# First attention: q, k and the score maxima in two fp32r parts, scores of 24 and 26 rows in four row tiles

## The reference

```python
qkv = x @ W_qkv
q, k, v = jnp.split(qkv, 3, axis=-1)           # 16 heads of 8 dims
scores = jnp.einsum('bhnd,bhmd->bhnm', q, k) / jnp.sqrt(jnp.float32(128))
attn = jax.nn.softmax(scores, axis=-1)
out = jnp.einsum('bhnm,bhmd->bhnd', attn, v)
x = _layernorm(x + out)
```

## Time and profile before

| | before |
|---|---|
| median of 3 runs | 1043.92 us (1043.27 to 1044.46) |
| span of the profiled execution | 1041.4 us |
| PE busy | 995.5 us (96%) |
| PEld busy | 475.4 us (46%) |
| DVE busy | 834.0 us (80%) |
| ACT busy | 729.9 us (70%) |
| POOL busy | 475.6 us (46%) |

### The profile page before, as it was taken

One profiled execution on the slowest core, in us unless ns is written; L12 is line 12 of the kernel. 1 busy time (PEld: TensorE's weight loads), 2 busy tenths in 40 slices (PEclk: granted clock), 3 DMA queues, 4 the chain that ended last, 5 costly groups with the idle time before them and its releaser, 6 DMA issues. The chain is left out here.

```text
span 1041.4 us, 20120 instructions
## 1 busy us (share of the span) xinstructions
PE 995.5 (96%) x5835; PEld 475.4 (46%) x5835; DVE 834.0 (80%) x1874; ACT 729.9 (70%) x939; POOL 475.6 (46%) x483
## 2 busy tenths in 40 slices
PE   8899999999999999999999999999999999999996
PEld 3222222222222235888888887873332333222485
DVE  6889999999999977787888789897666666643677
ACT  2078777787777786555555555568898888899754
POOL 0332514325053725676777677576442244220275
PEclk9999999999999999999999999999999999999998
DMA  6553222131321003344324323443512331230011
GB/s 198 153 186 119 76 76 89 44 117 46 96 78 52 3 2 101 102 128 145 101 91 156 121 90 117 137 137 102 172 65 61 121 119 63 60 122 1 1 31 52
DMA packets 73981, 97.04 MB, mean 93 GB/s; under 512 B 12669, under 2 KB 42237, under 8 KB 73533
## 3 DMA queue, kind: packets, MB, share of 16 engines
q1 hardware_dynamic: 73928, 96.40, 29.7%
HBM read 68.18 MB, written 27.79 MB: 92 GB/s over the span
## 5 line engine op out<-in xcount | busy, mean ns | idle before, releaser
L741 DVE TENSOR_REDUCE a_nmax<-a_ps_f 128x1 f32<-128x512 f32 x512 | 320.1, 683 | 20.2 <-PE a_ps_f L579 19.7
L497 ACT ACTIVATE a_prob<-a_ps_s 128x1024 f32<-128x1024 f32 x256 | 251.7, 1023 | 77.8 <-PE a_ps_s L646 76.5
L1367 ACT ACTIVATE a_prob<-a_ps_s 128x1024 f32<-128x1024 f32 x256 | 244.4, 1026 | 28.0 <-PE a_ps_s L1419 26.7
L2187 POOL TENSOR_TENSOR moe_hl<-moe_hid,moe_hh 128x512 fp32r<-128x512 f32 x134 | 173.9, 1303 | 84.3 <-ACT moe_hh L2068 84.2
L579 PE MATMUL a_ps_f<-a_ks,a_qs 48*128 48x512 bf16 x512 | 157.9, 386 | 11.8 <-DVE a_nmax L741 4.3
L2058 ACT ACTIVATE moe_ps<-moe_ps 128x512 f32<-128x512 f32 x128 | 74.5, 582 | 111.5 <-PE moe_ps L1981 110.7
L1432 PE MATMUL a_ps_o<-a_prob,a_va 128*32 128x512 f32 x1024 | 136.4, 605 | 1.4 <-DVE a_turned_o L1547 0.5
L659 PE MATMUL a_ps_o<-a_prob,a_va 128*32 128x512 f32 x1024 | 136.4, 605 | 0.5 <-ACT a_prob L497 0.4
L646 PE MATMUL a_ps_s<-a_qs,a_ks 51*128 51x512 bf16 x512 | 132.5, 381 | 1.7 <-ACT a_prob L497 1.5
L579 PEld LDWEIGHTS a_ps_f<-a_ks,a_qs 48*128 48x128 bf16 x512 | 39.7, 93 | 192.2 <-DVE a_nmax L741 162.2
L2109 DVE TENSOR_TENSOR moe_prod<-moe_cw,moe_ps 128x512 f32<-128x512 f32 x128 | 87.2, 681 | 27.4 <-PE moe_ps L1981 26.7
(11 more groups left out here) (302 smaller groups left out, 1640.1 us busy)
## 6 DMA issues: line engine op xcount, KB each, us to landing
moe_cw<-r_weights SPq DMA_DIRECT2D x256, 128.0 KB, 2.9
parts_q<-a_parts SPq DMA_DIRECT2D x48, 256.0 KB, 2.5
parts_k<-a_parts SPq DMA_DIRECT2D x48, 256.0 KB, 2.5
a_qs<-parts_q SPq DMA_DIRECT2D x126, 96.0 KB, 2.4
a_ks<-parts_k SPq DMA_DIRECT2D x126, 96.0 KB, 2.5
a_xt<-in_x_t SPq DMA_DIRECT2D x8, 256.0 KB, 2.8
out_x<-g_X SPq DMA_DIRECT2D x7, 256.0 KB, 2.3
moe_wg<-in_wg SPq DMA_DIRECT2D x1, 1088.0 KB, 6.6
```

What stands on the lines that cost most here:

```text
L497: nc.scalar.activation(prob[:, u % PSLOTS, :, :], ps_s[:, u % 2, :, :], ACT.Exp, scale=float(P) ** -0.5).then_inc(exp_done, 1)
L741: nc.vector.tensor_reduce(nmax[:, half_no, h % 2, col:col + 1], ps_f[:, bank, :], AX.X, ALU.max, negate=True).then_inc(max_done, 1)
L1367: nc.scalar.activation(prob[:, u % PSLOTS, :, :], ps_s[:, u % 2, :, :], ACT.Sigmoid, scale=float(HD) ** -0.5).then_inc(exp_done, 1)
L2187: nc.gpsimd.tensor_tensor(hl[:, part_at(j), :], hid[:, hid_at(j), :], hh[:, part_at(j), :], ALU.subtract).then_inc(hl_done, 1)
```

## The change

q and k are split into two fp32r parts instead of three bf16 parts, and the maxima too. Three pairs of parts remain (24 rows), and two rows of maxima (26). Four heads lie at partitions 0, 32, 64 and 96, so that scores run in four row tiles of 32. `s1_place` changes the order of the heads in the first pass: score n takes head (n + 2) mod 4 of its group. The stacks, the maxima and the selection become fp32r. A group's stack is read by four DMAs for q and four for k (24 rows of 2 KB each), parts are written by two DMAs, the maxima's rows by four. The rows of ones are filled by GpSimd ahead of the first stack, and SP lays them once more into the first group. At the start one selection gives four heads, by two matmuls for q and two for k; its matrix comes as fp32 and GpSimd turns it into fp32r. The V product, the maxima, the exponentials, the order of the units and the three banks stay as they are. The core of the diff:

```diff
 def s1_place(n):
-    return 2 * (n // (2 * NT)) + n % 2, n // 2 % NT
+    return HG * (n // (HG * NT)) + (n + 2) % HG, n // HG % NT

+def quarter_rows(tile, h, n_rows):
+    return tile[QTR * (h % HG):QTR * (h % HG) + n_rows, h // HG, :]
+
+def write_terms(sp, scratch, parts, n, done):
+    dst, src = scratch.rearrange("r p t -> p r t"), parts.bitcast(F32)
+    if n == 0:
+        sp.dma_start(dst[:, 0:2, :], src[:, 0:1, :].broadcast_to([P, 2, T])).then_inc(done, 16)
+        sp.dma_start(dst[:, 2:3, :], src[:, 1:2, :]).then_inc(done, 16)
...
+def read_terms(sp, scratch, dst, grp, done):
+    for i in range(HG):
+        src = bass.AP(tensor=scratch.tensor, offset=(i * NG + grp) * T, ap=[[H * T, FQKR], [1, T]])
+        sp.dma_start(dst[QTR * i:QTR * i + FQKR, grp, :].bitcast(F32), src).then_inc(done, 16)
+
+def split_in_two(eng, ops, src, parts, k, split, parts_done, zero):
+    ops.tensor_tensor(parts[:, 0, :], src, zero, ALU.add).then_inc(split, 1)
+    eng.wait_ge(split, k + 1)
+    ops.tensor_tensor(parts[:, 1, :], src, parts[:, 0, :], ALU.subtract).then_inc(parts_done, 1)
...
             def max_rows(b, p, half_no):
-                for i in range(2):
-                    sp.dma_start(qs[p][HALF * i + QKR:HALF * i + MXR, half_no * HH // 2:(half_no + 1) * HH // 2, :],
-                                 mparts[i * PARTS * HH * NT // 2:(i + 1) * PARTS * HH * NT // 2, :]).then_inc(max_in, 16)
+                rows = MAX_ROWS // HG
+                for i in range(HG):
+                    src = rows_of(half_no).start + i * rows
+                    dst = qs[p][QTR * i + FQKR:QTR * i + FMXR, half_no * NG // 2:(half_no + 1) * NG // 2, :]
+                    sp.dma_start(dst.bitcast(F32), mparts[src:src + rows, :]).then_inc(max_in, 16)
...
-                nc.tensor.matmul(ps_f[:, bank, :], stack_rows(qs[p], h, QKR)[:, qt * P:(qt + 1) * P],
-                                 stack_rows(ks[p], h, QKR), start=True, stop=True).then_inc(s1_done, 1)
+                nc.tensor.matmul(ps_f[:, bank, :], quarter_rows(qs[p], h, FQKR)[:, qt * P:(qt + 1) * P],
+                                 quarter_rows(ks[p], h, FQKR), start=True, stop=True).then_inc(s1_done, 1)
...
-                    mm = nc.tensor.matmul(ps_s[:, u % 2, i, :], stack_rows(ks[p], h, MXR)[:, kt * P:(kt + 1) * P],
-                                          stack_rows(qs[p], h, MXR), start=True, stop=True)
+                    mm = nc.tensor.matmul(ps_s[:, u % 2, i, :], quarter_rows(ks[p], h, FMXR)[:, kt * P:(kt + 1) * P],
+                                          quarter_rows(qs[p], h, FMXR), start=True, stop=True)
...
+            for i in range(2):
+                nc.gpsimd.memset(ks[i][:, :, :].bitcast(F32), 1.0).then_inc(filled, 1)
+            nc.gpsimd.memset(msplit[:, :, :, :, :], 0.0).then_inc(mt_chain, 1)
+            pool.wait_ge(select_in, 16)
+            nc.gpsimd.tensor_tensor(sel[:, :, :, :], sel_in, g["zero"][:, :].unsqueeze(2).unsqueeze(3).broadcast_to(
+                [P, 2, 2, PLACED_ROWS]), ALU.add).then_inc(sel_done, 1)
...
-                nc.gpsimd.tensor_tensor(msplit[:, :, 0, :], src, zero, ALU.add).then_inc(mt_chain, 1)
-                pool.wait_ge(mt_chain, 3 * k + 1)
-                nc.gpsimd.tensor_tensor(mrest[:, :, :], src, msplit[:, :, 0, :], ALU.subtract).then_inc(mt_chain, 1)
-                pool.wait_ge(mt_chain, 3 * k + 2)
-                nc.gpsimd.tensor_tensor(msplit[:, :, 1, :], mrest[:, :, :], zero, ALU.add).then_inc(mt_chain, 1)
-                pool.wait_ge(mt_chain, 3 * k + 3)
-                nc.gpsimd.tensor_tensor(msplit[:, :, 2, :], mrest[:, :, :], msplit[:, :, 1, :],
+                nc.gpsimd.tensor_tensor(dst[:, :, 0, :], src, zero, ALU.add).then_inc(mt_chain, 1)
+                pool.wait_ge(mt_chain, k + 2)
+                nc.gpsimd.tensor_tensor(dst[:, :, 1, :], src, msplit[:, half_no, :, 0, :],
                                         ALU.subtract).then_inc(mt_parts, 1)
```

More of the change, by code:

```diff
@@ L30 @@
 QKR = PAIRS * HD
-MXR = QKR + PARTS
 HALF = P // 2
+TERMS = 3
+QTR = P // HG
+S1_HALF = H * NT // 2
+FQKR = TERMS * HD
+FMXR = FQKR + 2
+PLACED_ROWS = P - QTR + FQKR
+MAX_ROWS = 2 * S1_HALF
 PAIR_DIMS = HD // 2
@@ L53 @@
 WARM = (5, 2, 3)
-PLACED = 2
 RC, CW_EARLY = 8, 3
@@ L350, in attention0 @@
         first_out = [sem(f"first_out{n}") for n in "qk"]
[L351 to L353 removed]
+        first_done, first_high, first_low = (sem("first_" + n) for n in ("done", "high", "low"))
+        select_in, sel_done, placed, filled = sem("select_in"), sem("sel_done"), sem("placed"), sem("filled")
         s1_done, max_done = sem("s1_done"), sem("max_done")
@@ L522, in _ @@
                     act.wait_ge(first_done, 2 * n + i + 1)
[L523 to L529, removed]
-                act.wait_ge(first_done, 4 + (1, 3, 4)[k])
-                nc.scalar.activation((qs, ks)[n][0][0:HALF + QKR, j, :], ps_s[0:HALF + QKR, n, j, :],
-                                     ACT.Copy).then_inc(placed[j], 1)
+                    nc.scalar.activation(parts[n][:, 0, in_half(i)], ps_s[:, n, i, 0:T // 2], ACT.Copy).then_inc(first_high, 1)
+            act.wait_ge(filled, 2)
+            act.wait_ge(first_done, 4 + 1)
+            nc.scalar.activation(qs[0][0:PLACED_ROWS, 0, :], ps_s[0:PLACED_ROWS, 0, 0, :], ACT.Copy).then_inc(placed, 1)
             act.wait_ge(cleared, 5)
@@ L701, in _ @@
             pe.sem_inc(k_done, 1)
-            pe.sem_inc(stack_in[0], 64)
+            pe.sem_inc(stack_in[0], 128)
             warm_up(WARM[1])
-            pe.wait_ge(select_in, 16)
-            pe.wait_ge(first_rest, 4)
-            for j in range(PLACED):
-                for n in range(2):
-                    if j == 0:
-                        pe.wait_ge(first_mid, 2 * n + 2)
-                        pe.wait_ge(first_low, 2 * n + 2)
-                    for k, a in enumerate((2 * n, 1, 2 - 2 * n)):
-                        mm = nc.tensor.matmul(ps_s[0:HALF + QKR, n, j, :], sel[:, n, a, j, :], parts[:, n, a, :],
-                                              start=(k == 0), stop=(k == PARTS - 1))
-                    mm.then_inc(first_done, 1)
+            pe.wait_ge(sel_done, 1)
+            for n in range(2):
+                pe.wait_ge(first_high, 2 * n + 2)
+                pe.wait_ge(first_low, 2 * n + 2)
+                for a in range(2):
+                    mm = nc.tensor.matmul(ps_s[0:PLACED_ROWS, n, 0, :], sel[:, n, a, :], parts[n][:, a, :],
+                                          start=(a == 0), stop=(a == 1))
+                mm.then_inc(first_done, 1)
             pe.wait_ge(g["consts_in"], 16)
@@ L825, in split_qk @@
                 pool.wait_ge((q_taken, k_taken)[n], b + 1)
-                split_in_parts(pool, nc.gpsimd, qk[:, n, :], rest[:, n, :], parts[:, n, :, :], 2 * b + n, split,
-                               parts_done, g["zero"][:, :].broadcast_to([P, T]))
+                split_in_two(pool, nc.gpsimd, qk[:, n, :], parts[n][:, :, :], 2 * b + n, split, parts_done,
+                             g["zero"][:, :].broadcast_to([P, T]))
             def units(b, p, u0, u1, qk_on, fore, back, tail):
@@ L2517, in layouts @@
     dims, at = np.divmod(np.arange(P), H)
-    heads = at % HH * 2 + at // HH
+    heads = at % NG * HG + at // NG
     order = heads * HD + dims
@@ L2521, in layouts @@
     r["w_qkv"] = np.ascontiguousarray(np.concatenate([w[:, :P][:, order], w[:, P:2 * P][:, order], w[:, 2 * P:]], 1))
-    select = np.zeros((P, 2, PARTS, PLACED, HALF + QKR), dtype=np.float32)
-    for n, pairs in enumerate(((0, 1, 0, 1, 0, 2), (1, 1, 2, 2, 0, 2))):
-        for j in range(PLACED):
-            for half in range(2):
-                for r_at, part in enumerate(pairs):
-                    for d in range(HD):
-                        select[d * H + half * HH + j, n, part, j, HALF * half + r_at * HD + d] = 1.0
-    r["select"] = select.reshape(P, -1).astype("bfloat16")
+    select = np.zeros((P, 2, 2, PLACED_ROWS), dtype=np.float32)
+    for n, parts in enumerate(((0, 0, 1), (0, 1, 0))):
+        for j in range(HG):
+            for r_at, part in enumerate(parts):
+                for d in range(HD):
+                    select[d * H + j * NG, n, part, QTR * j + r_at * HD + d] = 1.0
+    r["select"] = select.reshape(P, -1)
+    heads = at % HH * 2 + at // HH
     r["gate_t"] = np.ascontiguousarray(np.asarray(i["L0_ffn_gate_weight"]).T)
```

103 lines of the change are left out of this document (53 added, 50 removed).

## The result

The changed kernel takes 1269.14 us (median of 4 executions, 1261.26 to 1271.47) beside 1043.77 us for the kernel before: a ratio of 1.214, 95% interval 1.2097 to 1.2184. The forecast was 1072 us, range 1042 to 1080: slower, as forecast, but by 225 us in place of 28, far outside the range. The profiled execution took 1271.47 us with a span of 1269.6.

A forecast was written before the change was run, and what follows sets the result against it. It took the first attention as latency-bound by a closed 2.48 us loop through VectorE's maximum, two lone scores and the V product. 1043.9 + 26.3 - 0.5 + 2.2 gave 1072 us, range 1042 to 1080.

The forecast's parts named there:

- part 1: First attention: two lone first-pass scores per group, as fp32r, each end 117 ns later; 2.48 to 2.71 us, 114 groups, +26.3 us.
- the loop: First-attention group: VectorE's maximum, a lone first-pass score, the V product, another lone score, back to the maximum; 2.48 us before.
- The near row: L1405, fp32r 128x128 against 512 columns: load 186 ns, matmul 503, taken as the price of 24-row scores.
- Four row tiles: First-attention scores on four row tiles, not two: could save one 0.23 us round per group, but beside the loop: 0.
- GpSimd: GpSimd's splits per batch fall from 12 to 6 instructions, the maxima's from 8 to 4: 0 in steady state.
- Start: Before the second pass: earlier first score, later x, half the GpSimd work from there; -0.5 us, bounds -3 and +2.
- SP's queue: More DMA issues delay the second half's maxima, so batch 0's unit 16 second-pass scores wait: +2.2 us once, bounds 0 and 4.
- The last burst: After 367.6 us, second pass without maxima: first load exposed (+0.115), second round (0.23) may go; 0, within 2 us.
- (a): Rival: a 24-row fp32r load is as cheap as a 48-row bf16 one; 1046 us, 1042 to 1048, chance 0.10.
- (b): Rival: V product's loads get in earlier, so the group sinks to VectorE's floor of 2.40 us; 1037 us, chance 0.07.
- (d): Rival: one of the two lone score loads per first-attention group is covered after all; 1059 us, chance 0.08.
- (c): Rival: 4-byte scores on different row tiles do not overlap, 0.59 us more per group; 1113 us, chance 0.08.

## Why the prediction was wrong, point by point

**The step that failed** is one that the text never took: it priced every instruction at a granted clock of 1.00. The earlier trace rows showed 1.00 for the work before, the durations of part 1 came from rows at that level, and I carried both over to work with half the rows, without a rival in which the clock moves. Of the 221.5 us in seven batches, 7 x (47.66 - 44.15) = 24.6 are the change at 1.00, and the other 197 are the clock. At 1.00 the priced mechanism was right, and that is not luck: the period came out at 2.70 for 2.71, each part as told. The path is the loop itself: 2.70 at 1.00 becomes 4.16, because three of its four parts run on TensorE.

The Trainium skill, "TensorE: Matmul & The Clock Gate", section "Part 1: The HAM clock gate", ties the gate to how busy the engine has been. By the busy time of the profile this trace doesn't agree: TensorE was busy for 511.90 of 537.28 us at 0.50, and for 49.65 of 50 with 12 rows, also at 0.50. What the gate takes for busy no run here shows, but by the runs with other rows it is not this busy time.

1. Lone scores: +26.3 forecast, 114 groups of 2.71. At 1.00 the group is 2.70, part for part (0.43, 0.99, 0.53, 0.75), and a batch 3.51 longer, 28 us in eight. The near row was the right one: 181 ns for a load of 24 rows, 186 at 128. The Trainium skill's section "LDWEIGHTS" on the same page (columns, not rows, set a load's time) agrees with these two rows.
2. Four row tiles: 0 forecast. In steady groups right; in groups with other products 1.6 us a batch against two row tiles of the same type, which I had missed because I read one steady group only. It is inside the 47.66.
3. GpSimd: 0, right. It starts nothing late in the steady part.
4. Start: -0.5 forecast. The steps came as described: first score 1.55 us earlier, x 5.06 later, the splits from 36.23 (35 to 36.5 forecast), the turned maxima at 41.63 (40.4 to 41.8). Rows of the changed kernel, by engine, which answer to the earlier trace rows:

```profile
25.23 0.85 SPq L487 DMA_DIRECT2D g_X<-in_x  x1
...
36.23 1.04 POOL L300 TENSOR_TENSOR a_parts<-a_qk,g_zero 128x512 fp32r<-128x512 f32 x1 [29.67 <-DMA g_X<-in_x]
...
41.63 0.45 PE L589 MATMUL a_ps_f<-g_ident,a_msplit 128*128 128x128 f32 x1 [2.24 <-POOL a_msplit L841]
```

   Then the low clock behind that wait (6.8 us in place of 3.4) made the first second-pass score 2.0 later, the upper bound of +2.
5. SP's queue: +2.2 forecast, as a wait of second-pass scores for maxima. The queue ran late as described (the rows of maxima at 73.19, 73.9 forecast), but at the lower clock nobody waits for it. In the run with products at the start, at 1.00, the delay shows as a wait of the q product for its x, 0.74 us, and not for the maxima. The place was wrong, the size a third of the forecast and within the bounds:

```profile
73.74 1.12 PE L601 MATMUL a_ps_f<-a_xt,a_w 128*128 128x512 f32 x2 [0.74 <-DMA a_xt<-in_x_t]
```

6. The last burst: 0 within 2 us. The last batch is 4.6 us longer, its first 11 us at the lower clock.

At 1.00 throughout, 1043.8 + 24.6 + 2.35 + up to 4.6 would be 1071 to 1075 us (an estimate from these rows, not a run). The rivals: (a) fell with the loads at 181 ns; (b) and (d) with the group of 2.70 at 1.00, where both lone scores cost; (c) with scores that start within 0.02 us of each other. None had the time that came, and the bounds were of costs at one clock.

What stays open: what sets off a fall. In the kernels with few rows it came with the start of the second pass in most, and in one 140 us into it without a wait that differs from others. How the four-byte type adds to the rows, and the part of each pass, wasn't told apart.

## What to carry to other kernels

A duration read off a trace holds at the clock of its row. Where a change packs the same product into fewer rows of the array, give the other clock a chance and a price of its own: here every us at 0.50 cost 0.37 us (28.5 of 76.2 a batch). A loop found by its four parts in one group predicted the new period to 0.01 us, but an edit that shortens such a loop must also be followed through the groups that other work sets.

## What the runs showed of the hardware

- TensorE's granted clock was at 0.50 for 543 us of the first attention with the engine busy for 95% of the time (scores of 24 and 26 rows, fp32r, four row tiles). In bf16 with the same rows and tiles it was low in the second pass for 27 and 7 us. In the kernel before (bf16, two row tiles) it was low for 498 us with 12 rows, for 106, 10 and 3 us with 24, and in no batch of the traces with 36 and with all rows. With 56 and 58 rows of fp32r it was low in no batch of the trace.
- The same groups ran at either level: 1.00 for 120 us in one run and 0.50 for 543 in another.
- With two added full-array products of 0.21 us in a group, the profiled execution of the changed kernel had 1.00 in all batches, for 3.7 us a batch.
- At 0.50, scores in row tiles of 32 and of 64 rows started 0.55 us apart at the nearest, where four of one size start within 0.02 us on four tiles.
- A V product cut into two halves of its columns took 2 x 0.57 us at 1.00, the whole 1.00.
